# Gated cross attention with a mixture of rank-16 adapters: the order of work where one resident weight set follows another

## The reference

```python
x = x + tanh(g_xattn) * attention(layernorm(x), ctx)   # 32 query heads, 8 key/value heads of 128,
                                                       # rmsnorm on queries and keys, softmax(q k / sqrt(128) + mask)
x = x + tanh(g_ffn) * adapters(layernorm(x))

def adapters(x):                                       # 64 experts of rank 16, 16 chosen for each token
    scores = x @ Wr.T
    top_vals, top_idx = top_k(scores, 16)
    G = scatter(softmax(top_vals), top_idx)
    h = einsum('nd,krd->nkr', x, A)
    return 2.0 * einsum('nkr,kdr->nd', h * G[:, :, None], B)
```

## Time and profile before

| | |
|---|---|
| median of 3 runs | 2399.37 us (2396.16 to 2401.35) |
| profiled execution | 2401.17 us |
| its span | 2399.4 us |
| TensorE matmul busy | 2289.7 us, 95% of the span |
| VectorE busy | 1614.7 us, 67% |
| GpSimd busy | 1313.9 us, 55% |
| ScalarE busy | 1179.2 us, 49% |
| mean granted clock of TensorE | 0.982 |

### The profile page before, as it was taken

How to read it: one execution, slowest core, us unless ns; L and a number is a source line. 1 busy time by engine, 2 the same in 40 slices (tenths; PEclk the granted TensorE clock), 3 DMA queues, 4 the chain that set the end, 5 groups by cost and what they waited for, 6 DMA issues and landing times.

```text
span 2399.4 us, 35662 instructions
## 1 busy us (share of the span) xinstructions
PE 2289.7 (95%) x11600; PEld 1924.3 (80%) x11600; DVE 1614.7 (67%) x2651; ACT 1179.2 (49%) x3763; POOL 1313.9 (55%) x1811
## 2 busy tenths in 40 slices
PE   5998998999999989999999699999899999999899
PEld 4886887888888878888888588788787787788687
DVE  6557457777777787777777745755756877644755
ACT  4455545666666676666666622422423334333421
POOL 5566567655555575555555344654645655343421
PEclk8999999999999999999999799999999999999999
DMA  4687546757767457742233444545546357324653
GB/s 169 217 229 271 179 158 235 207 165 203 191 167 210 126 175 194 196 135 88 90 95 114 146 159 158 210 167 173 195 159 245 129 204 264 113 81 131 231 174 132
DMA packets 180231, 412.98 MB, mean 172 GB/s; under 512 B 12176, under 2 KB 77968, under 8 KB 164624
## 3 DMA queue, kind: packets, MB, share of 16 engines
q1 hardware_dynamic: 176016, 381.34, 46.6%
q0 software_dynamic: 4032, 29.36, 6.9%
HBM read 293.21 MB, written 176.16 MB: 196 GB/s over the span
## 4 chain that ended last, share of the span: by engine, by line
PE 88%; DVE 3%; issue 3%; POOL 3%; DMA 2%; ACT 1%; SPq 0%; POOLq 0%; ACTq 0%; DVEq 0%
PE bank L706 24%; PE bank L708 24%; PE bank L707 24%; PE bank L764 4%; PE bank L772 2%; PE bank L752 2%; DVE t_lo L1226 1%; PE bank L787 1%; PE bank L789 1%; PE bank L788 1%; DVE s_lo L1226 1%; DMA staged<-in_w_q 1%; PE bank L740 1%; PE bank L723 1%; PE bank L804 1%
## 5 line engine op out<-in xcount | busy, mean ns | idle before, releaser
L706 PE MATMUL bank<-t_hi,s_hi 128*128 128x512 f32 x2688 | 1091.1, 406 | 74.8 <-issue 42.4
L708 PE MATMUL bank<-t_hi,s_lo 128*128 128x512 f32 x2688 | 1059.3, 394 | 0.0
L707 PE MATMUL bank<-t_lo,s_hi 128*128 128x512 f32 x2688 | 1056.9, 393 | 0.0
L706 PEld LDWEIGHTS bank<-t_hi,s_hi 128*128 128x128 f32 x2688 | 510.9, 190 | 182.5 <-issue 82.9
L1226 DVE TENSOR_TENSOR s_lo<-staged,s_hi 128x512 fp32r<-128x512 f32 x672 | 539.9, 848 | 98.9 <-ACT s_hi L954 91.3
L708 PEld LDWEIGHTS bank<-t_hi,s_lo 128*128 128x128 f32 x2688 | 509.3, 189 | 112.1
L707 PEld LDWEIGHTS bank<-t_lo,s_hi 128*128 128x128 f32 x2688 | 511.4, 190 | 91.4
L954 ACT CAST s_hi<-staged 128x512 fp32r<-128x512 f32 x448 | 258.3, 623 | 359.3 <-DMA staged<-heads 190.0
L1646 POOL TENSOR_SCALAR small<-small 128x4 f32<-128x4 f32 (+1 forms) x192 | 65.5, 341 | 417.7 <-ACT small L1039 338.0
L1661 POOL TENSOR_TENSOR staged<-staged 128x512 f32<-128x512 f32 x96 | 136.9, 1426 | 257.3 <-DMA staged<-gated 86.1
L1735 POOL TENSOR_TENSOR sums<-sums,usum 128x512 f32<-128x512 f32 x64 | 97.1, 1538 | 210.5 <-DVE usum L1240 188.7
(11 more groups left out here) (126 smaller groups left out, 2981.1 us busy)
## 6 DMA issues: line engine op xcount, KB each, us to landing
heads<-heads SPq DMA_DIRECT2D x128, 256.0 KB, 3.7
t_raw<-combos SPq DMA_DIRECT2D x28, 1024.0 KB, 8.5
t_raw<-in_sets SPq DMA_DIRECT2D x25, 1024.0 KB, 8.2
staged<-in_w_q SPq DMA_DIRECT2D x32, 768.0 KB, 5.7
staged<-heads SPq DMA_DIRECT2D x32, 768.0 KB, 5.8
sums<-sums SPq DMA_DIRECT2D x18, 1024.0 KB, 7.9
sums<-sums SPq DMA_DIRECT2D x36, 512.0 KB, 4.7
xt<-x_columns SPq DMA_DIRECT2D x8, 1792.0 KB, 7.3
```

The lines of the kernel that those rows point to most:

```text
L706: nc.tensor.matmul(out, s_hi[w][:, cols], high, start=start, stop=False, skip_group_check=True)
L707: nc.tensor.matmul(out, s_hi[w][:, cols], low, start=False, stop=False, skip_group_check=True)
L708: done = nc.tensor.matmul(out, s_lo[w][:, cols], high, start=False, stop=at == 3, skip_group_check=True)
```

## The change

`FILL_POSITIONS` becomes (2, 3, 4, 5, 6, 7, 8), for the seven turns into sets 1, 2, 5, 6, 7, 8 and 9. In the three loops of SyncE in which these turns lie, `stage` now stands in front of `refill` in beat 1, so it comes between the refills of slots 0 and 1; away from a turn `refill` does nothing, and the order is the same as before.

```diff
-FILL_POSITIONS = (4, 5, 6, 7, 9, 10, 11)
+FILL_POSITIONS = (2, 3, 4, 5, 6, 7, 8)
 FILL_POSITIONS_QUERY = (2, 4, 5, 6, 7, 8, 9)
...
         for e in range(KV0, QA0):
             for j in SEVEN:
-                refill(e, entries[e].ks[j])
                 if j == 1:
                     stage(e + 1, e)
+                refill(e, entries[e].ks[j])
...
             for j in SEVEN:
-                refill(e, j)
                 if j == 0 and q == 0:
                     sums_in(0)
...
                 if j == 1:
                     stage(e + 1, e)
-                    if q and sums_stored(q - 1):
-                        sums_out(q - 1)
+                refill(e, j)
+                if j == 1 and q and sums_stored(q - 1):
+                    sums_out(q - 1)
...
         for e in range(A0, B0):
             for j in SEVEN:
-                refill(e, j)
                 if j == 1:
                     stage(e + 1, e)
+                refill(e, j)
```

## The result

| | before | after |
|---|---|---|
| median (12 runs each) | 2400.35 us | 2395.61 us (2390.48 to 2398.97) |
| ratio | | 0.998, 95% interval 0.9973 to 0.9988 |
| profiled span | 2399.4 us | 2394.6 us |
| mean granted clock | 0.982 | 0.978 |

The account below looks back on a forecast made before the run. VectorE was taken to bound the kernel at turns, TensorE elsewhere. Three plain turns 4.8, entries 8, 16, 82, 90: 3.6 - 0.7 + 2.0 + 3.5, total 13.2 us: 2401.2 to 2388.0 profiled, median 2386, range 2375 to 2402.

Parts of the forecast that it names:

- Entry 8: Turn into entry 8: product 8.0 starts at 209 to 210, not 202.9, yet 3.6 us gained, bounds 6 gained, 1 lost.
- entry 16: Turn into entry 16: normalised rows come 2.6 us later, 1.9 come back; 0.7 us lost, between 0 and 3.
- the 20 to 21 that were to show the forecast right: Sign at the plain turn: entry 66 takes 20 to 21 us although product 66.0 is 4 to 5 us late.
- the 22 that were to show it wrong: Sign: entries 58, 66, 74 taking 22 us or more after that late start mean VectorE is still the bound.
- the 1.5 us wait before 66.5: Entry 66: product 66.5 waits 1.5 us, to 1711.9, for bank 2, whose combination stands behind low half 6.
- the clock's term: Plain turn: half speed loses 1.4 us or more, counted as 0.1, leaving 1.6 gained a turn, 4.8 for three.
- both costs in full: Worst bound for one plain turn: 2 us lost; the best bound was 3.3 gained.
- The term of entry 90: Turn into entry 90: product 90.0 0.8 us late, 91.0 at about 2256.5, not 2260.4; 3.5 gained, between 7 and 0.
- The term of entry 82: Turn into entry 82: product 82.0 at 2031, not 2024.9; end 2058.3 against 2060.0; 2.0 us gained, between 5 gained and 4 lost.
- The wait is not paid back: Slower rival: late first products, collisions still stretch VectorE, half clock lost in full; 10 us lost, 2409; chance 0.20.
- Order matters little: Rival: VectorE's work sets a turn's length in either order, the seven turns cancel; 2399, give or take 3; chance 0.15.
- My best ends: Sum over all seven turns of each part's best bound: 28 us gained; worst ends 14 lost.

Follow-up runs that it names:

- kernel 3: The change plus 40 transposes of the identity into an unused bank on TensorE ahead of entries 58, 66 and 74: 2387.9 us, ratio 0.9949.
- Kernel 6: The change, but with slot 1's refill ahead of the streamed tile again in the loop of entries 82 to 89: 2392.2 us, ratio 0.9970.
- kernel 1: The kernel before with the change's new positions alone, SyncE's order of transfers as before: 2389.4 us, ratio 0.9952.
- kernels 4 and 10: 4: kernel before with positions (2,3,5,6,7,8,9), 2373.9 us; 10: the change with (2,5,5,6,7,8,9), but into entry 90 4's positions and old transfer order, 2372.9 us.
- kernel 7: The change with positions (2,3,5,6,7,8,9) instead, its order of transfers kept: 2381.4 us, ratio 0.9928.

## Why the prediction was right about the sign and wrong about the size

**Right.** VectorE bounded the turns. Low half 0 went into idle time. The tile's transfer was issued 1 us ahead of slot 1's refill and no earlier than before. Slot 1 came late, and with it ScalarE and VectorE: 4.87 us idle for 4.3 forecast, product 66.0 5.5 us late for 4.8. GpSimd's second sum took 1.28 us. The half clock came at all three plain turns. Entry 8 (3.6 gained, measured 3.5) came out by its working, product 8.0 at 209.8; so did entry 16 (0.7 lost, measured 0.5: 2.4 lost ahead of it for 2.6, 1.9 given back inside it for 1.9). Product 82.0 was 6.8 us late where 6.1 were forecast. Entries 58, 66 and 74 took 21.4, 21.5 and 21.6 us, between the 20 to 21 that were to show the forecast right and the 22 that were to show it wrong. The total kept its sign because of entry 8: the other six turns gained 0.8 us together.

**The step that failed at the plain turns** is this one: "Nearly all of it falls into the 1.5 us wait before 66.5, so I count 0.1." Product 66.0 took 4.7 us in the change and 2.9 in kernel 3, 1.8 lost to the half clock, and kernel 3 shows that 1.6 of them reach the end of the entry. The wait that was to cover them was smaller than forecast, 0.5 us with the clock up and not 1.5: VectorE's low halves ran in 2.28 us each there, where the working had stretched them. And it does not stand still while TensorE is slow: the copy of product 66.0, the high half of slot 5 behind it and the low halves after them are pushed back too, so in the change 0.3 us of that wait are left. The other two deviations cancel each other: product 66.0 came 0.7 us later than forecast, and entry 66 with the clock up (19.9 us, kernel 3) was 0.7 shorter. So 1.6 for a turn, less the 1.5 by which the clock's term was too small, leaves the 0.1 measured at two of three; the third gained 1.1, since the kernel before had taken 46.8 there and not 46.1. The bound was in the prediction ("both costs in full"), and so was the rule of the Trainium skill (TensorE: Matmul & The Clock Gate, "HAM oscillation — how this bites in real kernels") that a wait between two bursts of matmuls lets the next burst start at the lower clock. The traces of the change agree with it at every plain turn: at product 66.0 the granted clock was 0.50 for 6.8 us, from within an idleness of 5.3 us on. I took the value that the wait seemed to cover, without asking whether what ends the wait hangs on the slow product itself.

**The term of entry 90** (3.5 gained, measured 0.6 lost) failed at the transfers. The working took "Slots 1 and 2 are done by 2227.3, product 90.0 starts 0.8 late". That is 23.1 us after the start of entry 89; slot 2's low half ended 25.7 after it, and product 90.0 came 2.8 us later than before. So the time taken for slot 2 was 2.6 us too early: its transfer, the last to land, took 11.4 us. Kernel 6 undoes the swap there: slot 2 is split 2.8 us earlier, product 90.0 starts 2.4 us earlier, and the turn gains 2.5 us against the kernel before. The swap itself accounts for 1.3 to 2.0 us of the miss, over entries 89 and 90 and as kernel 3 or the change is compared with kernel 6. Another 1.2 is entry 91, whose first product ran at half clock in the change. The rest is not separated.

**The term of entry 82** (2.0 gained, measured 0.5): product 82.0 is 0.7 later than forecast, and the entry takes 27.7 us, the first 4.5 of them at half clock, where 27.3 were counted. Here no experiment separates the parts; kernel 1, with the same positions and slot 1 first, takes 78.7 us for the three entries, and kernel 3, which differs in nothing there, 79.1. Two terms of the sum also left their own working: it gives 1.7 gained for entry 82, taken as 2.0, and 3.9 for entry 90, taken as 3.5.

**The rivals.** "The wait is not paid back" had the half clock right (1.7 in full, measured 1.6) and the collisions wrong: VectorE's work in entry 66 fell from 26.6 to 19.1 us. "Order matters little" gave 2399, give or take 3, near the measured 2395.6, but for a reason that kernels 4 and 10 refute: the order of this work is worth up to 28 us. My best ends added up to 28 us for this change; such a gain exists, but in another order.

## What to carry to other kernels

Work put forward into another engine's idle time is free only if its data has landed by then: ask for each place in an in-order list what lands last ahead of it, and what queues behind. When two transfers change places, work out anew when the ones behind them land. Count a lower TensorE clock after a long wait in full unless the wait that is to cover it is independent of the slow product. A list of positions and the order of the transfers that feed them are one decision: vary them together and by single beats, since one beat here was worth 15 us.

## What was not expected of the hardware

- Which of two engines pays for a collision cannot be told from the recorded starts. In the change GpSimd's sum starts at 1704.18, while a low half of the tile is running on VectorE, and VectorE's next low half at 1704.53 takes 3.38 us instead of 2.28. In kernel 3 the same three operations start with the same distances (the sum at 1701.61, the low half 0.36 us behind it), but there the low half takes 2.28, and the two sums together take 5.03 instead of 4.87. At 1685.71 VectorE's low half began 0.78 us before a sum of GpSimd ended, and is 0.66 longer. The Trainium skill (SBUF — State Buffer, "SBUF: two separate sides") describes a port pair that the one who starts first holds for its whole instruction. The rows of the change agree; those of kernel 3 show the later one by the recorded starts go through unhindered, and nothing here shows why.
- After 5.3 us without a matmul product 66.0 ran at 1.2 GHz; in kernel 3, with transposes in between and 0.78 us of idleness, it ran at 2.4 GHz. In kernel 7 the length of the wait does not decide: product 58.0 after 2.97 us took 4.3 us, product 66.0 after 3.04 us took 2.9. TensorE at the first matmul of each:

```profile
1526.72 0.79 PE L706 MATMUL bank<-t_hi,s_hi 128*128 128x512 f32 x1 [2.97 <-DVE s_lo L1226]
...
1684.81 0.50 PE L706 MATMUL bank<-t_hi,s_hi 128*128 128x512 f32 x1 [3.04 <-DVE s_lo L1226]
```
